# An audio tower on one core: state products by strips, between-block products round the columns, level copies by halves, a new order of the steps

## The reference

```python
h = layernorm(x); xx = shifted by one frame
q, k, v, g = mixes of h and xx, times Wq, Wk, Wv, Wg   # g a sigmoid
q = exp(rmsnorm(q)); k = exp(rmsnorm(k))
def step(carry, inp):              # the scan, per head, over the frames
    A = lam[..., None] * A + kt[..., None] * vt[..., None, :]
    z = lam * z + kt
    St = einsum('bhi,bhij->bhj', qt, A); Zt = einsum('bhi,bhi->bh', qt, z)
x = x + (g * S / Z) @ Wo.T
x = x + gelu(layernorm(x) @ W1.T) @ W2.T
```

## Time and profile before

| | us |
|---|---|
| median of 3 runs | 1223.17 (1221.0 to 1224.21) |
| the profiled execution's own time | 1218.9 |
| its span, first to last instruction | 1217.1 |
| PE, DVE, ACT, POOL busy | 1138.9, 986.5, 621.5, 300.9 |
| mean granted clock of PE | 0.990 |

### The profile page before, as it was taken

One profiled execution on the slowest core, in us unless ns is written; L12 is line 12 of the kernel. 1 busy time (PEld: TensorE's weight loads), 2 busy tenths in 40 slices (PEclk: granted clock), 3 DMA queues, 4 the chain that ended last, 5 costly groups with the idle time before them and its releaser, 6 DMA issues.

```text
span 1217.1 us, 43497 instructions
## 1 busy us (share of the span) xinstructions
PE 1138.9 (94%) x17955; PEld 807.8 (66%) x17955; DVE 986.5 (81%) x3362; ACT 621.5 (51%) x1100; POOL 300.9 (25%) x174
## 2 busy tenths in 40 slices
PE   4799999999999999999999999999999999999997
PEld 4576676666767676766666667666676766667664
DVE  7878788797887979788796887979879797987962
ACT  3346446363554736446363554736446364554634
POOL 4123131221403223131311403223131221403211
PEclk8799999999999999999999999999999999999999
DMA  5321313222141312313222141312313222141210
...
DMA packets 51492, 91.48 MB, mean 75 GB/s; under 512 B 9536, under 2 KB 26592, under 8 KB 51296
## 3 DMA queue, kind: packets, MB, share of 16 engines
...
...
## 4 chain that ended last, share of the span: by engine, by line
PE 83%; DVE 9%; POOL 4%; issue 3%; ACT 2%; DVEq 0%; POOLq 0%
PE bank L1056 10%; PE bank L1049 9%; PE bank L1084 9%; PE bank L1078 8%; PE bank L919 8%; PE bank L914 7%; PE bank L1014 7%; PE bank L998 5%; PE bank L990 4%; PE bank L1033 4%; POOL nrm L391 3%; PE bank L1029 3%; PE bank L954 3%; PE bank L943 2%; PE bank L994 2%
## 5 line engine op out<-in xcount | busy, mean ns | idle before, releaser
L514 ACT ACTIVATE px<-bank 128x512 f32<-128x512 f32 (+1 forms) x128 | 72.8, 569 | 218.0 <-PE bank L998 152.9
L763 DVE COPY_PREDICATED px<-mask,bank 128x512 f32<-128x512 uint32 (+1 forms) x128 | 88.6, 692 | 79.6 <-issue 76.8
L1078 PE MATMUL bank<-xa,f1w 128*128 128x512 f32 (+1 forms) x256 | 124.7, 587 | 14.8 <-DVE qtok L704 13.0
L1056 PE MATMUL bank<-w,hid 128*128 128x128 f32 x1024 | 121.9, 277 | 17.2 <-ACT hid L533 17.2
L1056 PEld LDWEIGHTS bank<-w,hid 128*128 128x128 f32 x1024 | 116.7, 192 | 31.6 <-ACT hid L533 31.6
L1014 PEld LDWEIGHTS bank<-qx,ki 128*32 128x32 f32 x7680 | 89.6, 110 | 42.3 <-issue 33.9
L827 DVE TENSOR_TENSOR ki<-k,rp 128x96 f32<-128x96 f32 (+13 forms) x512 | 113.2, 295 | 0.6 <-ACT k L499 0.6
L397 POOL TENSOR_TENSOR ab<-af,heads 128x896 f32<-128x896 f32 x16 | 40.8, 2552 | 291.1 <-DVE af L755 291.1
L1049 PE MATMUL bank<-c,w 128*128 128x512 f32 (+1 forms) x256 | 111.4, 568 | 1.1 <-ACT c L527 0.9
L1084 PE MATMUL bank<-hid,f2w 128*128 128x512 f32 (+1 forms) x256 | 107.5, 563 | 0.0
L1014 PE MATMUL bank<-qx,ki 128*32 128x16 f32 x7680 | 99.2, 193 | 6.9 <-issue 6.6
...
## 6 DMA issues: line engine op xcount, KB each, us to landing
qx<-qq SPq DMA_DIRECT2D x256, 96.0 KB
...
```

The lines of the kernel that those rows point to most:

```text
L763: V.copy_predicated(px[c % 2][0:n, :, 0:n], mask[0:n, 0:n].rearrange("p (o m) -> p o m", o=1).to_broadcast([n, HEADS, n]), bank[DIAG][0:n, ...
L1056: last = mm(dst[:, P * i:P * i + P], hid[:, j, P * m:P * m + P], w2[:, j, :], start=(j == 0), stop=(j == 3))
L1078: mm(dst[:, 0:width[g]], f1w[:, P * j:P * j + P], xa[:, cols(g)], start=True, stop=True).then_inc(f1_ok, 1)
```

## The change

1. `LAST` becomes 3 and every `body` gets a new order and new lags; `USES` follows. Only SP has steps at lag 3.
2. `pairs_a`: the 64-column product becomes two of 32 columns over all 64 moving columns and comes first, then `kw[:, 0]`, then `ko` with `j` outside and window inside.
3. `scan`: the state product becomes four, one for each head's 32 columns.
4. `klevels` and `qlev` work on halves of the clip; `ki`, `ko` and `kw` then hold one half, and `last_pairs` waits for all of the half before.
5. At the start only the columns behind the clip's end are cleared, `qq` and `qc` not at all, and `ki`, `ko`, `kw` ahead of their first use. `vec` is loaded behind `xT`.

```diff
-LAST = 2
+LAST = 3
...
+
+    if g:
+        eng.wait_ge(pb_ok, nth(b, TILES, TILES // 2))
+    else:
+        before(eng, pb_ok, b, TILES, TILES)
...
         before(sp, dct_ok, b, 2, 2)
         sp.dma_start(xT[:, 0:full], A["xT"][b, :, :]).then_inc(x_in, 16)
+        if first(b):
+            sp.wait_ge(s_zero, 1)
         sp.dma_start(xT[0:TAIL, full:T], A["xtail"][b, :].rearrange("(p o) -> p o", o=1)).then_inc(x_in, 16)
         if first(b):
+            sp.dma_start(vec[:, :], A["vec"]).then_inc(s_vec, 16)
             weights()
     def expert(b):
...
             sp.wait_ge(s_init, 2)
-        sp.wait_ge(ql_ok, nth(b, GROUPS, g + 1))
+        sp.wait_ge(ql_ok, nth(b, 2, g // 2 + 1))
...
+            spread(b, 0); hand_h2(b); hand_v(b); spread(b, 1)
+        if (b := at(1)) is not None:
+            hand_h1(b)
+        if (b := at(2)) is not None:
+            spread(b, 2); hand_gate(b)
         if (b := at(0)) is not None:
             samples(b)
...
+        if (b := at(2)) is not None:
+            spread(b, 3)
+        if (b := at(3)) is not None:
+            store(b, 0)
+        if (b := at(2)) is not None:
             expert(b)
```

Clears and waits (POOL; ACT's `exps`; DVE):

```diff
-    gp.memset(xT[:, :], 0.0).then_inc(s_zero, 1)
+    gp.memset(xT[:, full:PADT], 0.0).then_inc(s_zero, 1)
     gp.memset(nhalf[:, :], -0.5)
     gp.memset(phalf[:, :], 0.5)
-    gp.memset(zq[:, :], 1.0)
-    for tile in (hl, mixed[0], mixed[1]):
-        gp.memset(tile[:, :], 0.0)
+    gp.memset(zq[:, T:PADT], 1.0)
+    gp.memset(hl[:, 0:1], 0.0)
+    for tile in (mixed[0], mixed[1]):
+        gp.memset(tile[:, T:PADT], 0.0)
...
-            before(act, kin_ok, b, GROUPS, GROUPS)
-            before(act, kon_ok, b, GROUPS, GROUPS)
+            before(act, kin_ok, b, 2, g + 1)
+            before(act, kon_ok, b, 2, g + 1)
...
-    for tile in (k, qc, ga, gate_f, c1, xa):
-        V.memset(tile[:, :], 0.0)
-    for tile in (qq, ki, ko, kw):
-        last = V.memset(tile[:, :, :], 0.0)
+    for tile in (k, ga, gate_f, c1, xa):
+        last = V.memset(tile[:, T:PADT], 0.0)
```

Levels:

```diff
-        dve.wait_ge(eq, nth(b, 2, g // 2 + 1))
+        dve.wait_ge(eq, nth(b, 2, g + 1))
         for at, m, skip in ((Q8, EIGHT, 0), (Q32, 2 * WIN, WIN), (Q64, P, P // 2)):
-            w = scan_w[g] if m == EIGHT else GRP
             n = m - skip
-            last = V.tensor_tensor(qq[:, g, at:at + w * n // m].rearrange("p (x m) -> p x m", m=n),
-                                   q[:, g, 0:w].rearrange("p (x m) -> p x m", m=m)[:, :, skip:m],
-                                   over(pw[:, 0:n], w // m, n), ALU.mult)
+            last = V.tensor_tensor(qq[:, 2 * g:2 * g + 2, at:at + GRP * n // m].rearrange("p o (x m) -> p o x m", m=n),
+                                   q[:, 2 * g:2 * g + 2, :].rearrange("p o (x m) -> p o x m", m=m)[:, :, :, skip:m],
+                                   pw[:, 0:n].rearrange("p (o x m) -> p o x m", o=1, x=1).to_broadcast([P, 2, GRP // m, n]), ALU.mult)
         last.then_inc(ql_ok, 1)
...
-        dve.wait_ge(ek, nth(b, 2, g // 2 + 1))
-        last_use(dve, b, g)
+        dve.wait_ge(ek, nth(b, 2, g + 1))
+        last_pairs(dve, b, g)
         for dst, m, n, ref in parts:
-            w = scan_w[g] if m <= WIN else GRP
+            w = HALF if m > WIN else min(HALF, WINS * WIN - HALF * g)
             view = lambda ap: ap.rearrange("p (x m) -> p x m", m=m)[:, :, 0:n]
-            last = V.tensor_tensor(view(dst[:, GRP * (g % 2):GRP * (g % 2) + w]), view(k[:, GRP * g:GRP * g + w]),
+            last = V.tensor_tensor(view(dst[:, 0:w]), view(k[:, HALF * g:HALF * g + w]),
                                      over(rp[:, P - ref:P - ref + n], w // m, n), ALU.mult)
         last.then_inc(done, 1)
     def inside(b, g):
+        if first(b) and g == 0:
+            V.memset(ki[:, :, :], 0.0).then_inc(s_lev, 1)
+            dve.wait_ge(s_lev, 1)
         klevels(b, g, [(ki[:, j, :], EIGHT, j + 1, j) for j in range(EIGHT)], kin_ok)
     def between(b, g):
+        if first(b) and g == 0:
+            V.memset(ko[:, :, :], 0.0)
+            V.memset(kw[:, :, :], 0.0).then_inc(s_lvo, 1)
+            dve.wait_ge(s_lvo, 1)
         parts = [(ko[:, j - 1, :], WIN, EIGHT * j, EIGHT * j) for j in range(1, NE)]
         klevels(b, g, parts + [(kw[:, 0, :], 2 * WIN, WIN, WIN), (kw[:, 1, :], P, P // 2, P // 2)], kon_ok)
```

Products:

```diff
-        O, k0, o = by_head(bank[BETWEEN][:, :]), GRP * (c // 2 % 2) + P * (c % 2), c % 2
+        O, k0, o = by_head(bank[BETWEEN][:, :]), P * (c % 4), c % 2
...
-            pe.wait_ge(kon_ok, nth(b, GROUPS, g + 1))
-        for w in range(n):
-            r, t0 = slice(WIN * w, WIN * w + WIN), P * o + WIN * w
-            for j in range(1, NE):
-                t = EIGHT * j
-                last = mm(O[r, :, WIN * w + t:WIN * w + t + EIGHT], ko[:, j - 1, k0 + WIN * w:k0 + WIN * w + WIN],
-                          x[:, :, Q8 + t0 + t:Q8 + t0 + t + EIGHT], start=True, stop=True)
+            pe.wait_ge(kon_ok, nth(b, 2, c // 4 + 1))
+
+        if n == NW:
+            t0 = Q64 + P // 2 * o
+            for w in (0, 1):
+                r = slice(WIN * w, WIN * w + WIN)
+                mm(O[r, :, P // 2:P], kw[:, 1, k0 + WIN * w:k0 + WIN * w + WIN], x[:, :, t0:t0 + P // 2], start=True, stop=True)
         for w in range(0, n, 2):
             t0 = Q32 + P // 2 * o + WIN * (w // 2)
-            last = mm(O[WIN * w:WIN * w + WIN, :, WIN * w + WIN:WIN * w + 2 * WIN], kw[:, 0, k0 + WIN * w:k0 + WIN * w + WIN],
-                      x[:, :, t0:t0 + WIN], start=True, stop=True)
-        if n == NW:
-            t0 = Q64 + P // 2 * o
-            last = mm(O[0:P // 2, :, P // 2:P], kw[:, 1, k0:k0 + P // 2], x[:, :, t0:t0 + P // 2], start=True, stop=True)
+            mm(O[WIN * w:WIN * w + WIN, :, WIN * w + WIN:WIN * w + 2 * WIN], kw[:, 0, k0 + WIN * w:k0 + WIN * w + WIN],
+               x[:, :, t0:t0 + WIN], start=True, stop=True)
+        for j in range(1, NE):
+            for w in range(n):
+                t0 = P * o + WIN * w + EIGHT * j
+                last = mm(O[WIN * w:WIN * w + WIN, :, WIN * w + EIGHT * j:WIN * w + EIGHT * j + EIGHT],
+                          ko[:, j - 1, k0 + WIN * w:k0 + WIN * w + WIN], x[:, :, Q8 + t0:Q8 + t0 + EIGHT], start=True, stop=True)
         last.then_inc(pa_ok, 1)
...
-        D, k0 = by_head(bank[DIAG][:, :]), GRP * (c // 2 % 2) + P * (c % 2)
...
-            pe.wait_ge(kin_ok, nth(b, GROUPS, c // 2 + 1))
+            pe.wait_ge(kin_ok, nth(b, 2, c // 4 + 1))
...
         if c:
-            mm(S[:, s0:s0 + n], ab[:, c - 1, :], qc[:, P * c:P * c + n], start=True, stop=False, skip_group_check=True)
+
+            for hd in range(HEADS):
+                r = slice(HD * hd, HD * hd + HD)
+                mm(S[r, s0:s0 + n], ab[:, c - 1, r], qc[:, P * c:P * c + n], start=True, stop=False, skip_group_check=True)
         pe.wait_ge(px_ok, nth(b, TILES, c + 1))
         for hd in range(HEADS):
             r = slice(HD * hd, HD * hd + HD)
```

The five changing banks (`USES`), each name with its lag:

```diff
+    [("w2_0", 2), ("w1_11", 2), ("qT0", 1), ("nmT0", 2), ("at0", 2), ("f1_01", 2), ("zt", 1), ("f1_10", 2), ("rT1", 1), ("f1_12", 2), ("oT1", 2), ("wo1", 1), ("w1_03", 1)],
+    [("n2T1", 2), ("w1_10", 2), ("w1_13", 2), ("w2_1", 2), ("v1", 1), ("n1T1", 2), ("f2_0", 2), ("nT1", 0), ("q0", 0)],
+    [("dct0", 0), ("w1_12", 2), ("v0", 1), ("qT1", 1), ("f1_00", 2), ("u", 1), ("at1", 2), ("rT0", 1), ("f1_13", 2), ("f2_1", 2), ("n2T0", 1), ("q1", 0)],
+    [("k1", 1), ("g0", 1), ("g1", 1), ("f1_02", 2), ("f1_11", 2), ("oT0", 2), ("w1_00", 1), ("w1_02", 1)],
+    [("k0", 1), ("kT0", 1), ("n1T0", 2), ("kT1", 1), ("dct1", 0), ("nmT1", 2), ("f1_03", 2), ("nT0", 0), ("wo0", 1), ("w1_01", 1)],
```

More of the change, by code:

```diff
@@ L570, in body @@
+                if (b := at(2)) is not None:
+                    gelu2(b, 1, 2); gelu2(b, 1, 3)
+                if (b := at(0)) is not None:
+                    hlT(b, 1)
                 if (b := at(1)) is not None:
@@ new lines, in body @@
+                if (b := at(0)) is not None:
+                    normed(b)
+                if (b := at(1)) is not None:
+                    between(b, 1); gate(b, 0); gate(b, 1); merge(b, 3); inside(b, 1)
+                if (b := at(0)) is not None:
+                    shifted(b)
+                if (b := at(1)) is not None:
+                    gated(b, 0)
+                if (b := at(0)) is not None:
+                    mixes(b, 0)
+                if (b := at(2)) is not None:
+                    result(b, 0)
@@ new lines, in body @@
+                if (b := at(2)) is not None:
+                    nmTs(b, 1); n1Ts(b, 1)
+                if (b := at(1)) is not None:
+                    zts(b)
+                if (b := at(2)) is not None:
+                    ats(b, 1); f1s(b, 0, 3)
+                if (b := at(1)) is not None:
+                    pairs_b(b, 2); pairs_a(b, 3); scan(b, 1); pairs_b(b, 3)
+                if (b := at(2)) is not None:
+                    f1s(b, 1, 0); f1s(b, 1, 1)
+                if (b := at(1)) is not None:
```

(5 more changed lines are left out.)

297 lines of the change are left out of this document (140 added, 157 removed), and 5 rows, old and new, of the table USES.

## The result

| | before | after |
|---|---|---|
| median, us (4 runs each, same chip) | 1223.69 | **1148.15** |
| lowest, highest | 1221.0, 1228.81 | 1143.93, 1151.89 |
| ratio, 95% interval | | **0.9377**, 0.9329 to 0.9425 |
| span of the profiled execution | 1217.1 | 1150.0 |

The forecast was 1108 (1080 to 1158): right in its sign and inside the range, but 40 us of the expected 115 did not come. These lines of the page answer to the earlier trace rows; the clock line has a digit for each fortieth of the span, and the queue line gives packets, MB and share.

A forecast was written before the change was run, and what follows sets the result against it. TensorE was taken as the bound, VectorE not far behind. Work 63.2 + engine waits 1.1 + "issue" 1.2 = 65.5 us a round; 84.7 + 15 x 65.5 - 4 + 40 = 1103 span, giving 1108 us (1080 to 1158).

The forecast's parts named there:

- the waits stay: Rival: the old round's 4.0 us of waits for engines remain; 68.4 us a round, median 1152; chance 0.22.
- (a): `pairs_a`: overlapping strips make a chunk 0.90 us, before 1.09 without two emptyings; seven chunks, -1.3 us a round.
- (b): State product as four strips: 0.24 us like the `v` strips; four behind narrow work give -0.4 us a round.
- strips in a row: Rival: long strips don't run side by side; +7.6 us a round, 73.1, median near 1223; chance 0.04.
- (c): TensorE's changes of tile shape: 35 a round become 12, -2.2 us; fewer late second loads, -0.3.
- (d): TensorE's waits a round: engines from 4.0 us to 1.1, "issue" left at 1.2.
- (e): VectorE: 32 instructions fewer a round, -2 us; busy 58.6 of 65.5, no cost while TensorE's queue is longer.
- (f): ACT: up to four table loads a round instead of two, +2.6 us on ACT; expected cost 0, uncovered +2.6.
- (g): SyncE: `hand_h1` ahead of `spread(b, 2)` delays that transfer some 2 us; expected cost 0, uncovered 2 a round.
- open turn-round: Rival: level buffers `ki`, `ko`, `kw` refill in the open; 73.8 us a round, median 1234; chance 0.04.
- (h): Start and end: start net -1 us, bounds -2 and +4; last full round -4; behind the mark -0.5.

The follow-up runs named there:

- e6: e5 with the clears of `ki`, `ko` and `kw` moved ahead of VectorE's first `shifted()`: 1147.55 us, ratio 0.9398 to the kernel before.
- e3: Changed kernel with the old product forms put back (`pairs_a` by windows, state as one product of 128 rows): 1177.19 us, ratio 0.9627 to before.
- e12: Changed kernel with early clears and only the second part of its narrow stretch broken up by wide products: 1130.46 us, ratio 0.9258 to before.
- e1: Changed kernel with half of `pairs_b`'s instructions over the same columns, leaving out odd columns' own factor: 1080.51 us, ratio 0.8836 to before.
- e2: Changed kernel with every product of `pairs_b` issued twice: 1390.01 us, ratio 1.1375 to before.
- e4: Kernel before with the two new product forms alone (state by strips, `pairs_a` round the columns): 1228.77 us, ratio 1.0059 to before.
- e5: Changed kernel with TensorE's order alone changed, no narrow batch over 227 instructions: 1153.82 us, ratio 0.9437 to before.
- e7: Changed kernel with its state product as one of 128 rows again: 1147.37 us, ratio 0.9382 to before.
- e8: Changed kernel with early clears and a middle TensorE order, batches of at most 340 instructions: 1146.76 us, ratio 0.9373 to before.

## Why the prediction was right, and where it was not

**The frame.** `w1s(0, 0)` starts at 82.96 before and 89.38 after for clip 0, and at 1106.51 after for clip 15. So 1150.0 = 89.4 + 15 x 67.8 + 43.5, where the forecast's 1103 is, from the same mark, 82.0 + (15 x 65.5 - 4) + 42.7. The rounds are 39 us too long, the start 7, the end 1. By its own sign the prediction was wrong here: "I am wrong if the period is above 67", and it is 67.8. The measured time lies in the range because that was stretched to 68.8 a round for a rival, "the waits stay", whose cause did not hold.

**(a), (b) forms: right, a little better.** These rows show a `pairs_a` chunk and, further on, a state product with the `v` strips behind it:

```profile
666.35 0.41 PE L1027 MATMUL bank<-qx,kw 128*32 128x256 f32 x2
666.37 0.41 PE L1030 MATMUL bank<-qx,kw 128*32 128x128 f32 x2
666.59 0.39 PE L1027 MATMUL bank<-qx,kw 128*32 128x256 f32 x2
...
667.18 0.74 PE L1005 MATMUL bank<-v_f,kcT 128*32 128x32 f32 x55
```

```profile
686.57 0.43 PE L1070 MATMUL bank<-qc,ab 128*32 128x128 f32 x8
686.82 0.40 PE L1074 MATMUL bank<-px,v 128*32 128x128 f32 x8
```

The chunk lasts 666.35 to 667.18 = 0.83 us (forecast 0.90), since the first load doesn't stand in the open; the state takes 0.25 (0.24). So the rival of strips in a row is out. The Trainium skill's rule that was weighed there (TensorE: Matmul & The Clock Gate, The mechanism: a weight load overlaps only where the row group differs) does not describe these rows: strips share all 128 rows.

**(c) shapes: right.** The trace has 35 changes a round before and 12 after, as counted. The best round, 64.51 with two waits of 0.5 us together in it, leaves 64, or 63.5 with the prediction's 0.25 for each wait, against my 63.2 of work.

**(d) waits: this step failed, in its second half.** "1.1 for engines": the waits for engines are 6.3 us from 110 us on, 0.4 a round, less than forecast. "I leave 'issue' at 1.2, since the program doesn't get shorter": I took "issue" as a constant per program, though it is a matter of how fast instructions are used up. `pairs_b` uses 129 of them in 0.58 us. "issue" rose by 28.8 us (the view counts from the modelled end; with the 0.25 of the prediction for each of 24 more stops, 35). And each of the five longest stops (1.8 us and more in the view) was followed by a stretch at half clock; with two others, 1.6 and 2.0 us behind the start of a `zts`, these are seven stretches and 27.3 us, worth 14: a cost that no step had. With 8 less for engines than forecast, 35 + 14 - 8 is some 40 against the 39 found. The time thus fell where the rival "the waits stay" had it, 1152, but that rival was wrong: its waits for ACT and DVE went, others came. That the two times agree is chance.

**(e) DVE: right,** 57.0 to 58.1 of busy time a round (58.6), 3.3 less than the 60.8 of before where I took 2; of the 52 us lost in all, 7 are clears at the start. It never became the bound.

**(f) ACT tables: wrong in number, harmless.** The loads in after (us in total, mean ns | idle):

```profile
L508 ACT ACT_TABLE_LOAD x15 | 19.2, 1283 | 0.3
...
L564 ACT ACT_TABLE_LOAD x15 | 19.2, 1283 | 0.3
```

```profile
728.77 1.28 ACT L564 ACT_TABLE_LOAD   x1
730.06 0.69 ACT L564 ACTIVATE hid<-bank,f1b 128x512 f32<-128x512 f32 x1
```

Two a round, 32 with the first and last, as before: `tanhs` behind `gelu2` needs none. A load takes 1.28 us again and the activation starts 0.01 behind it. The drain that the Trainium skill has behind a load (ScalarE: Activation LUTs, What ACT_TABLE_LOAD costs) does not show in this row either.

**(g) hand_h1, and the open turn-round: right.** No wait of TensorE over the view's threshold for `ko`, `kw`, `ki` or `qx` after the first clip.

**(h) start: wrong by 7 us.** I let the clears hide "where queues wait on a lone clip's chain anyway" and bounded them at +4. TensorE stood 6.1 us for `ki`, and e6 won those 6 us with the clears in VectorE's 10 us of waiting for `hl`:

```profile
PE bank L1052 <- DVE ki L847: 6.1, 1, 6.1
```

**What stays open.** What sets the pace of the packets, and a better rule than the 298 instructions in 3.85 us: with it FETCH met the time of e3 and came within 5 us in e12, but missed by 16 to 87 us in e1, e2, e4, e5, e7 and e8; whether a stop alone or only with slow products behind it brings the clock down: behind the changed kernel's five longest stops it fell each time, in e4 behind some of the like only (not behind the longest of all, 2.8 us), at `zts` after far less. Some 0.4 us a round of e5 isn't placed. The early clears were not run on the changed kernel by themselves.
